# TensorE's background of a chunk in one piece, and a second buffer for the recurrent state

## The reference

```python
def step(S, inp):                                  # S: state, 32 x 32 for each head
    qi, ki, vi, ei = inp
    kh = jnp.einsum('bchd,bhde->bche', ki, S)      # read of the state with the keys
    kh_hat = (kh - mean(kh)) * rstd(kh)
    g = w * kh_hat + b - (vi - ki);  gw = g * w
    v_new = (gw - mean(gw) - kh_hat * mean(gw * kh_hat)) * rstd(kh)
    A = tril(qi @ ki.T) * ei
    qh = jnp.einsum('bchd,bhde->bche', qi, S) - A @ v_new
    o = qi + _ln(qh, w, b)
    S = S - jnp.einsum('bchd,bche->bhde', ki * ei[..., None], v_new)
    return (S, o)
```

```python
q = silu(x @ Wq);  k = l2norm(x @ Wk);  v = x @ Wv;  beta = 2 * sigmoid(x @ Wbeta)
gate = x @ Wg1 @ Wg2
o = rmsnorm(o * sigmoid(gate)) * norm_w;  x = x + layernorm(o @ Wo)
x = x + layernorm((silu(x @ gate_w) * (x @ up_w)) @ down_w)       # widths 512, 1536, 512
```

## Time and profile before

| what | value |
|---|---|
| timed runs, median of 3 | 962.62 us (960.66 to 962.68) |
| the profiled execution | 958.5 us, of which the span of the trace is 956.7 us |
| PE, DVE, ACT, POOL busy in the span | 89%, 73%, 47%, 47% |
| PE's share of the chain that ended last | 76% |
| mean granted TensorE clock | 0.925 of full |

### The profile page before, as it was taken

The page is one execution under the profiler, slowest core; times in us unless marked ns, Lnnn a source line. Parts: engine busy times, 40 slices in busy tenths (PEclk is TensorE's granted clock), DMA queues, the critical chain, the costliest instruction groups (busy, mean ns, idle before and its releaser), DMA issues.

```text
span 956.7 us, 21197 instructions
## 1 busy us (share of the span) xinstructions
PE 854.6 (89%) x7480; PEld 612.8 (64%) x7480; DVE 700.0 (73%) x2751; ACT 453.6 (47%) x1242; POOL 448.4 (47%) x832
## 2 busy tenths in 40 slices
PE   6756677677999999999999999999999999979895
PEld 3435354354767767676777776767677676767684
DVE  2688888988767687767786777778776777677442
ACT  1524333343454646465655555555646464542322
POOL 5231441533545554646464555645565545436312
PEclk9785766767999999999999999999999999989998
DMA  7011112110000001000010001000100000001000
GB/s 263 21 58 56 56 45 76 47 46 32 2 24 1 23 2 46 2 23 2 1 46 23 1 2 46 2 23 2 46 2 23 2 30 17 1 2 45 1 23 22
DMA packets 16714, 28.37 MB, mean 30 GB/s; under 512 B 3520, under 2 KB 3520, under 8 KB 16608
## 3 DMA queue, kind: packets, MB, share of 16 engines
q1 hardware_dynamic: 16608, 27.02, 8.8%
HBM read 22.82 MB, written 4.19 MB: 28 GB/s over the span
## 4 chain that ended last, share of the span: by engine, by line
PE 76%; DVE 13%; POOL 4%; issue 3%; ACT 2%; DMA 1%; POOLq 0%; DVEq 0%; ACTq 0%
PE bank L373 18%; PE bank L512 16%; PE bank L543 10%; PE bank L496 6%; PE bank L475 6%; PE bank L482 4%; PE bank L452 4%; PE bank L379 4%; PE bank L461 2%; POOL rho L947 2%; PE bank L430 2%; PE bank L395 2%; PE bank L436 2%; DVE work L1219 1%; PE bank L400 1%
## 5 line engine op out<-in xcount | busy, mean ns | idle before, releaser
L947 POOL TENSOR_TENSOR rho<-sy,cst 128x2 f32<-128x2 f32 x128 | 89.5, 699 | 354.5 <-DVE sy L1192 354.5
L766 ACT ACTIVATE qhR<-bank 128x64 f32<-128x64 f32 x128 | 28.4, 222 | 198.1 <-PE bank L482 194.5
L475 PE MATMUL bank<-VX,BDkR 128*64 128x64 f32 x1024 | 61.5, 244 | 67.8 <-DVE VX L1228 67.2
L475 PEld LDWEIGHTS bank<-VX,BDkR 128*64 128x64 f32 x1024 | 43.7, 146 | 120.3 <-issue 66.5
L1235 DVE TENSOR_TENSOR SQ<-SQ,bank 128x128 f32<-128x128 f32 x128 | 36.9, 288 | 97.4 <-PE bank L475 96.3
L543 PE MATMUL bank<-DW,fh 128*128 128x512 f32 x192 | 88.0, 459 | 1.9 <-DVE fl L1302 1.9
L725 ACT ACTIVATE BDkR<-kR,cst 128x128 f32<-128x128 f32 x256 | 81.1, 393 | 0.1
L543 PE MATMUL bank<-DW,fl 128*128 128x512 f32 x192 | 76.4, 398 | 0.0
L1214 DVE SCALAR_TENSOR_TENSOR work<-work,rho,rR 128x32 f32<-128x32 f32 x256 | 53.2, 249 | 26.7 <-POOL rho L947 24.7
L1028 POOL TENSOR_TENSOR fl<-f,fh 128x512 fp32r<-128x512 f32 x32 | 45.7, 1428 | 53.1 <-ACT fh L664 29.9
L373 PE MATMUL bank<-Wq,xnT 128*128 128x512 f32 x128 | 67.5, 675 | 0.0
(11 more groups left out here) (169 smaller groups left out, 2164.2 us busy)
## 6 DMA issues: line engine op xcount, KB each, us to landing
xt<-in_x SPq DMA_DIRECT2D x16, 256.0 KB, 2.7
x<-in_x SPq DMA_DIRECT2D x16, 256.0 KB, 2.9
out<-x SPq DMA_DIRECT2D x16, 256.0 KB, 2.0
x<-in_gate_w SPq DMA_DIRECT2D x12, 256.0 KB, 2.7
x<-in_up_w SPq DMA_DIRECT2D x12, 256.0 KB, 2.7
xn<-in_down_w SPq DMA_DIRECT2D x12, 256.0 KB, 2.9
Wk<-in_wk SPq DMA_DIRECT2D x1, 1024.0 KB, 5.8
Wv<-in_wv SPq DMA_DIRECT2D x1, 1024.0 KB, 8.3
```

The lines of the kernel that those rows point to most:

```text
L475: ins = mm(dS[p, e], bdkr[:, gh, j % 4, p], VX[:, e], start=True, stop=True, skip_group_check=True)
L947: tt(dst, src, cst[:, C_NH:C_NH + n], ALU.pow).then_inc(*one)
```

## The change

- The state has two buffers, `SQ[0]` and `SQ[1]`, used in turn. The state add reads the one and writes the other, and `chunk_q` fills the queries of the next chunk's buffer.
- On TensorE, B moves ahead of the update: `write_state` is now the last step of every chunk, and the whole background stands in one piece between kh and the update. The queries' read qs (with its waits for `BDq` and for the take of the chunk before) moves from behind kh to between update and product, and reads the old buffer.
- On VectorE, in tiles 3 and on, the background (a new function `background`) moves ahead of the state add. In tiles 0 to 2 it stays behind. `prep_kss`, `fin_stats` and `prep_eta` stay behind the add throughout; in j=4 `ffn_f` now precedes `prep_kn` and `prep_d`.
- On ScalarE, in tiles 3 and on, j=5: `ffn_fh` of the second round and both halves of `prep_BDk` stand ahead of the take; before, `ffn_fh` and the second half came behind it.
- To make room, small buffers are shared: `Pw` with `t_`, `u` with `g`, one `sums` and one `roots` for the three norms of heads, two buffers of statistics for five.

The amount of work stays the same on TensorE and VectorE. The core of the diff:

```diff
-        SQ = sb("SQ", 4 * 48)
-        SQv = SQ[:, :].rearrange("p (g e) -> p g e", g=4)
-        S = SQv[:, :, CH:48]
+        SQ = [sb(f"SQ{n}", 4 * 48) for n in range(2)]
+        SQv = [b[:, :].rearrange("p (g e) -> p g e", g=4) for b in SQ]
+        S = [v[:, :, CH:48] for v in SQv]
...
-        scan_t = Steps(sem("scan_t"), "kh qs upd qa")
+        scan_t = Steps(sem("scan_t"), "kh upd qs qa")
...
                 ins.then_inc(*scan_t.one("kh"))
-                if j % 4 == 0:
-                    pe.wait_ge(diag_a.sem, diag_a.at(f"q{j // 4}", n))
-                if begun(c - 1):
-                    pe.wait_ge(scan_a.sem, scan_a.at("qh", c - 1))
-                for gh in range(2):
...
                 ins.then_inc(*scan_t.one("upd"))
+                if j % 4 == 0:
+                    pe.wait_ge(diag_a.sem, diag_a.at(f"q{j // 4}", n))
+                if begun(c - 1):
+                    pe.wait_ge(scan_a.sem, scan_a.at("qh", c - 1))
+                for gh in range(2):
...
                     if j == 7 and post:
                         post_wo(t - 1)
-                    if scan:
-                        write_state(t, j, s)
 
                     if j == 0 and 0 in ffn:
                         ffn_u(*ffn[0], 1)
...
                         if prep:
                             prep_brow(t + 1)
+                    if scan:
+                        write_state(t, j, s)
...
-                    if j == 5 and prep:
+                    if j == 5 and t >= 3:
+                        if 1 in ffn:
+                            ffn_fh(*ffn[1])
+                        if prep:
+                            prep_BDk(t + 1, o, 0)
+                            prep_BDk(t + 1, o, 1)
+                    if j == 5 and t < 3:
                         prep_BDk(t + 1, o, 0)
...
-                tt(S, S, dS.rearrange("p (g e) -> p g e", e=DH), ALU.add).then_inc(*scan_v.one("S"))
+                tt(S[(j + 1) % 2], S[j % 2], dS.rearrange("p (g e) -> p g e", e=DH), ALU.add).then_inc(*scan_v.one("S"))
...
+                    if t >= 3:
+                        background(t, s, h, j)
                     if scan:
                         scan_state(t, j)
...
+                    if t < 3:
+                        background(t, s, h, j)
+
+                    if j == 2 and prep:
+                        prep_kss(t + 1)
+                    if j == 6 and fin:
+                        fin_stats(h - 2, 0)
+                        fin_stats(h - 2, 1)
+                    if j == 7 and prep:
+                        prep_eta(t + 1, o)
```

More of the change, by code:

```diff
@@ L130, in build @@
         ATB = sb("ATB", P)
-        SQ = sb("SQ", 4 * 48)
-        SQv = SQ[:, :].rearrange("p (g e) -> p g e", g=4)
-        S = SQv[:, :, CH:48]
-        work = sb("work", 4 * 64)
-        Pw, u, g, t_ = (work[:, 64 * n:64 * (n + 1)] for n in range(4))
+        SQ = [sb(f"SQ{n}", 4 * 48) for n in range(2)]
+        SQv = [b[:, :].rearrange("p (g e) -> p g e", g=4) for b in SQ]
+        S = [v[:, :, CH:48] for v in SQv]
+        work = sb("work", 2 * 64)
+        Pw = t_ = work[:, 0:64]
+        u = g = work[:, 64:128]
         em = work[:, 0:P]
@@ L152, in build @@
         norms = ("p", "a", "f", "y0", "y1")
-        st = {n: sb(f"st_{n}", 6) for n in "paf"}
-        st.update({f"y{k}": sb(f"st_y{k}", 6) for k in range(2)})
+        st_one, st_two = sb("st_one", 6), sb("st_two", 6)
+        st = {n: st_two if n in ("f", "y1") else st_one for n in ("p", "a", "f", "y0", "y1")}
         mv = {n: sb(f"mv_{n}", 2) for n in norms}
@@ L159, in build @@
         nb = {n: sb(f"nb_{n}", 1) for n in norms}
-        kss, rk = sb("kss", H), sb("rk", H)
-        qss, rq = sb("qss", H), sb("rq", H)
-        oss, ro = sb("oss", H), sb("ro", H)
+        kss = qss = oss = sb("sums", H)
+        rk = rq = ro = sb("roots", H)
         pause = sb("pause", 1)
@@ L452, in read_state @@
                         ins = mm(KAv[gp * 64:(gp + 1) * 64, gh, 0:48], bdk(s)[:, gh * NC + j, gp, :],
[L453 removed]
+                                 SQv[c % 2][:, 2 * gh + gp, :], start=True, stop=True, skip_group_check=True)
                 ins.then_inc(*scan_t.one("kh"))
[L455 to L463 removed]
             def write_state(n, j, s):
@@ L477, in write_state @@
                 ins.then_inc(*scan_t.one("upd"))
+                if j % 4 == 0:
[3 more added lines that the diff above has]
+                for gh in range(2):
+                    for gp in range(2):
+                        ins = mm(QH[gp * 64:(gp + 1) * 64, gh * DH:(gh + 1) * DH], bdq[:, j // 4, 2 * gp + gh, j % 4, :],
+                                 S[c % 2][:, 2 * gh + gp, :], start=(gh == 0), stop=False, skip_group_check=True)
+                ins.then_inc(*scan_t.one("qs"))
                 for gh in range(2):
@@ L1341, in quantize, with background @@
                     .then_inc(s_quant, 1)
+            def background(t, s, h, j):
+                norm, prep, scan, post, tail = live(t)
+                o = 1 - s
+                fin = s and is_pair(h - 2)
+                ffn = rounds(t, s, h)
+                if j == 0:
+                    if tail and s:
+                        tail_x1(t - 2)
+                    if tail and not s:
+                        tail_stats(t - 2)
+                    if not s and is_pair(h - 3):
+                        fin_out(h - 3, 1)
+                if j == 1:
+                    if tail and not s:
+                        tail_x1(t - 2)
+                    if 0 in ffn:
+                        ffn_f(*ffn[0])
+                    if norm and s:
+                        x_stats(t + 2)
+                if j == 2:
+                    if s and is_pair(h - 1):
+                        pair_xl(h - 1)
+                    if 0 in ffn:
+                        ffn_fl(*ffn[0])
+                if j == 3:
+                    if prep:
+                        prep_qR(t + 1, o)
+                    if post:
+                        post_og(t - 1, o)
+                if j == 4:
+                    if 1 in ffn:
+                        ffn_f(*ffn[1])
+                    if prep:
+                        prep_kn(t + 1)
+                        prep_d(t + 1)
+                if j == 5:
+                    if norm and not s:
+                        x_stats(t + 2)
+                    if fin:
+                        fin_y(h - 2, 0)
+                        fin_y(h - 2, 1)
+                if j == 6:
+                    if post:
+                        post_ogT(t - 1)
+                    if prep:
+                        prep_bx(t + 1)
+                if j == 7:
+                    if 2 in ffn:
+                        ffn_f(*ffn[2])
+                    if post and not s:
+                        tail_stats(t - 1)
+                    if fin:
+                        fin_out(h - 2, 0)
             def body(t, s, h):
```

66 lines of the change are left out of this document (2 added, 64 removed).

## The result

| | before | after |
|---|---|---|
| timed runs, median of 14 | 962.12 us (960.17 to 963.47) | **965.75 us** (963.73 to 967.07) |
| the profiled execution (span) | 958.5 us (956.7) | 966.6 us (964.8) |
| granted TensorE clock, mean | 0.925 | 0.915 |

The ratio is 1.0037, 95% interval 1.0028 to 1.0045: **slower by 0.4%**, where a gain of 0.7% was forecast. The two profiled executions lie 8.1 us apart, the medians 3.6 us: the profiled execution of before was 3.6 us under its median. The prologue and tile 0 vary from run to run: in six kernels further down that share their code up to tile 2 (early_before, acts_ahead, acts_split, late_too, ends_before, j2_behind) the stretch ahead of tile 0 took 29.5 to 30.7 us and tiles 0 to 2 together 188.8 to 191.9.

A forecast was written before the change was run, and what follows sets the result against it. It took TensorE to bound tiles 4 to 14 and the chain through VectorE the first three tiles. Its terms, -16.0 + 0 + 3.9 - 4 + 7.2 + 3.5 - 1.5 = -6.9 us, gave a 955.7 us median, range 946 to 967.

The forecast's parts named there:

- Part 5: Tiles 0 to 2: beta's products ahead of the j=5 update delay VectorE; +3.5 us, bounds 0 and +9.
- rival 2: The early tiles take back all, with 0.05 us a chunk more behind the update: 965 us, chance 0.09.
- Part 1: TensorE, tiles 4 to 14: one piece of background saves changes of array shape, 0.20 us a chunk, -16.0 us.
- part 3: VectorE's background ahead of the state add, tiles 3 and on: late states +3.9 us, earlier TensorE idle time gone, -4 us.
- Part 2: State's path from update to next kh: 0.94 us against TensorE's own 0.95, so taken as 0.
- Part 4: ScalarE's work behind the take of QH makes TensorE wait, 0.26 us in j=6, 0.86 after xf: +7.2 us.
- Tile 3: The tile after the early three: no change in time expected, taken at 0.
- Tile 15: The last tile: ffn_down of j=4 hides in an idle stretch of TensorE, -1.5 us.
- Rival 1: VectorE becomes the bound, with the state add late by 0.2 us in the mean chunk: 971 us, chance 0.12.
- Rival 3: A change of array shape on TensorE costs nothing, so the merge saves 0: 971.7 us, chance 0.03.
- rival 4: The waits of parts 3 to 5 don't come: -21.5 us, 941 us, chance 0.10.
- rival 5: It comes out even, from smaller savings of 0.12 us a chunk: 962 us, chance 0.09.

The follow-up runs named there:

- early_before: The changed kernel with TensorE's order of before in tiles 0 to 2 (B behind the update, queries' read ahead of the background): 955.77 us.
- acts_ahead: early_before with ScalarE's tail_xf (j=1 of odd tiles) and prep_g1 (j=5) ahead of the copy of QH in tiles 3 and on: 948.73 us, ratio 0.9857.
- acts_split: acts_ahead with TensorE's second piece of background (B) behind the update in every tile: 960.91 us, ratio 0.9998 to the kernel before.
- late_too: acts_ahead with VectorE's background behind the state add in tile 15: 952.58 us.
- ends_before: acts_ahead with tile 15 as before the change on both TensorE and VectorE: 948.37 us.
- j2_behind: acts_ahead with VectorE's background behind the state add in one more chunk, tile 15, j=2: 944.41 us, ratio 0.983 to the kernel before.
- dve_behind: The changed kernel with VectorE's background behind the state add in all tiles: 985.64 us, ratio 1.0239 to the kernel before.
- early_split: The changed kernel with TensorE's B behind the update again in tiles 0 to 2: 957.38 us, ratio 0.9945 to the kernel before.

## Why the prediction was wrong, and where it was right

The forecast of the span was -6.9 us and +8.1 came, 15.0 us apart: 4.9 in tiles 0 to 2, 2.5 in tile 15, 2.3 in tiles 4 to 14, 1.8 in tile 3, and 3.5 ahead of tile 0 and in the rest. Of the last, 1.1 is no more than the runs vary by, and the 2.4 is there in some measure in all the changed kernels (the rest took 86.7 to 90.4 us in them); 1.7 of it is the Wo product at a lower clock, with no cause shown. Against the medians the miss is less, +3.6 for -6.9, for the reason given with the result.

- **Part 5, tiles 0 to 2: the step that failed, and the one that decided the sign.** The mechanism and its price at j=5 were right: the state add came 3.3 us later in each of the three tiles (3.4 said), the fronts of the next chunk 3.3, 2.6 and 3.3 us (2.75 said). The step that failed is "in j=6 and j=7 VectorE waited about a microsecond each for the update before, which takes a part back". Almost nothing was taken back (the fronts behind j=6 and j=7 moved by -0.7 to +0.4), because the change put cen ahead of the update just there. Tile 1, j=6 after:

```profile
149.88 2.08 PE L437 MATMUL bank<-xn_dv_rT,cst 128*128 128x512 f32 x2
151.89 0.70 PE L467 MATMUL bank<-VX,BDkR 128*64 128x64 f32 x8
...
152.63 0.29 DVE L1241 TENSOR_TENSOR SQ<-SQ,bank 128x128 f32<-128x128 f32 x1 [1.48 <-PE bank L467]
```

  VectorE comes late to this chunk by the delay of j=5, and still waits 1.48 us for the update (1.05 before), since cen holds TensorE for 2.0 us. "Some" is what the prediction gave for cen and brow. By the medians all of B behind the update gives 8.4 us back and beta alone 2.8, which leaves 5.6 for the others; in the traces 3.2 of this lies in tiles 0 to 2. The result, 8.4 us, lies at the upper bound of +9 (three times the delay and nothing given back), and rival 2 had that bound. At the +3.5 that was forecast, the median would have been about 960.9 us, just under that of before.
- **Part 1, the merge: right in its price, too high in its count.** -16.0 was taken, with +3.9 for the late states of part 3 that go with it: -12.1. The step from acts_split to acts_ahead measured -9.7, and -7.3 without the wait for `bt` in j=6, which is no matter of shapes. j=0, 1, 2 and j=7 of even tiles saved 0.15 to 0.22, as worked out. The 4.8 us that are missing lie in two places. j=6 was counted at 0.20 and saved 0.03 against before (2 us in the stage): in that chunk A and B meet at `prep_gate`, whose 32-row shape stands between them, so no change of shape goes away. The prediction had seen this for j=5 alone, which saved 0.02. And the late states cost some 6 us in place of 3.9 (part 3): j=3, held for even, saved 0.04 to 0.06 only, because VectorE's background is late by 0.14 there. That nothing is saved where the shape changes anyway speaks for the change of shape as the cause.
- **Part 2, the state's path: right.** 0.94 us from update to kh at full clock, as said. What wasn't seen is that the two paths are even only at full clock: at the lower level of the early tiles TensorE's is 1.55 against 1.16.
- **Part 3, VectorE ahead of the add: right for the steady tiles, but for j=3.** From update to kh, against 0.94, j=4 took some 0.21 us more (0.22 to 0.26 said), j=7 of odd tiles 0.44 (0.3), and j=3 0.14 (0): some 6 us in place of 3.9. In return 5.8 us came back and not 4, in j=3 of odd tiles and in j=0 (acts_split). Tiles 3 and 15 were not counted chunk by chunk, and both lost.
- **Part 4, ScalarE behind the take: right.** The waits show 0.80 for xf and 0.17 for bt; the chunks' lengths in acts_ahead give 0.86 (0.86 said) and 0.24 (0.26), 7.0 us for the two (7.2).
- **Tile 3 (0 said, +1.8 measured).** It has VectorE's new order but the low clock and full queue of the early tiles. Its j=0:

```profile
235.92 0.69 PE L467 MATMUL bank<-VX,BDkR 128*64 128x64 f32 x8 [5.32 <-DVE VX L1234]
...
238.31 0.26 DVE L1241 TENSOR_TENSOR SQ<-SQ,bank 128x128 f32<-128x128 f32 x1
...
238.72 0.67 PE L453 MATMUL bank<-SQ,BDk 128*64 128x48 f32 x8 [1.16 <-DVE SQ L1241]
```

The update came at once behind `VX`, the add 2.39 us behind it. The condition for the new order, that TensorE's background is longer than VectorE's, doesn't hold here; j=0 lost 1.3 us and j=4 1.2. With VectorE's order of before (dve_behind) both losses are gone (+0.02, -0.05), though j=3 and j=5 lose more. The tile as a whole also hangs on how the tiles ahead leave it: with this same order in it, it takes 53.2 us in early_split, where j=1 gives 0.8 us back.
- **Tile 15 (-1.5 said, +1.0 measured).** The saving in j=4 came (-1.59), but j=2, 3 and 5 lost 4.1 us together: 1.8 by the late state in j=2, most of the rest by a lower granted clock in j=3 and j=5, with no cause shown.

Of the rivals, 2 had the right cause in its first term, part 5 near +9. That its 965 us meet the measured 965.75 so closely is luck: its second term, 4 us in part 2, did not come, and losses in tile 3, in tile 15 and behind it stand in its place. Rival 1, VectorE as the bound of the steady tiles, didn't come: j=0, 1, 2, 5 and 6 stayed free. Rival 3, no cost of a change of shape, would have left acts_split and acts_ahead equal but for the wait in j=6, and they are 7.3 us apart in the other chunks of the stage. Against rival 4, the waits of parts 3 to 5 all came; against rival 5, the chunks that TensorE sets saved 0.15 to 0.22 us and not 0.12, and the loss lay elsewhere. The rule cited beside it (the Trainium skill, "TensorE: Matmul & The Clock Gate", Part 2), weight loads pulled ahead of the matmuls in flight, doesn't hide such a change here: those 7.3 us would be 0.

## What to carry to other kernels

An order that is right where one engine sets the time can be wrong where another does: before moving work ahead of a handoff, list for every stage which engine waits at that handoff, and keep the old order where the receiver is the bound. If a slack that is to "take back" a delay exists only because of the order that the change undoes, it must be counted at zero. When a change loses, put it back stage by stage: here a change that cost 0.4% became a gain of 1.7% once it was left out of three tiles and, on VectorE, of one chunk, and two operations on a third engine had been moved.
